# Two-layer gated cross-attention with experts: causal maxima in shared banks, one-hots by wide comparisons, two casts on ScalarE

## The reference

```python
x = x + tanh(g_xattn[0]) * L0_xattn(layernorm(x), ctx, ctx, mask, ...)  # 16 heads of 16, causal
x = x + tanh(g_ffn[0])   * L0_ffn(layernorm(x), ...)    # 32 experts, top 8, capacity 256
x = x + tanh(g_xattn[1]) * L1_xattn(layernorm(x), ctx, ctx, mask1, ...) # 16 heads, not causal
x = x + tanh(g_ffn[1])   * L1_ffn(layernorm(x), ...)    # 8 experts, top 2, capacity 1024

def L0_xattn(q, k, v, ...):
    scores = einsum('bhqd,bhkd->bhqk', q @ Wq + bq, k @ Wk + bk) / 4
    scores = where(tril(ones(S, S)), scores, finfo.min) + attention_mask
    return einsum('bhqk,bhkd->bhqd', softmax(scores), v @ Wv + bv) @ Wp + bp
```

## Time and profile before

| | |
|---|---|
| median of three runs | 2179.87 us (2171.82 to 2183.06) |
| the profiled execution's own time | 2182.45 us |
| its span in the profile | 2180.7 us |
| mean granted clock of TensorE | 0.923 of full speed |
| layer 0's attention, first to last maximum (L823) | 79.6 to 597.1 us |
| layer 1's attention, first score for maxima to last (L658) | 1021 to 1559 us |
| DVE sat idle for PE before L823 | 113.0 us |
| PE sat idle for DVE's L823 | 35.9 us |

### The profile page before, as it was taken

One profiled execution on the slowest core, in us unless ns is written; L12 is line 12 of the kernel. 1 busy time (PEld: TensorE's weight loads), 2 busy tenths in 40 slices (PEclk: granted clock), 3 DMA queues, 4 the chain that ended last, 5 costly groups with the idle time before them and its releaser, 6 DMA issues. The chain is left out here.

```text
span 2180.7 us, 30480 instructions
## 1 busy us (share of the span) xinstructions
PE 1843.1 (85%) x9979; PEld 1024.6 (47%) x9979; DVE 1138.2 (52%) x3758; ACT 862.8 (40%) x1780; POOL 598.0 (27%) x577
## 2 busy tenths in 40 slices
PE   2689899888872999916899999998971999999995
PEld 1345455444442777613334444443331566666664
DVE  3477778877855344433877877777521111112211
ACT  1356555555450322203376766665650111111110
POOL 1312111210001577723211331231112233333322
PEclk9799999998985999958899999999985999999998
DMA  3445454335221678733333324332013233333314
GB/s 93 151 123 160 130 168 130 112 98 160 72 72 46 158 169 170 141 66 113 120 98 113 116 83 120 114 106 67 32 49 84 83 76 76 74 77 78 70 27 97
DMA packets 204252, 222.88 MB, mean 102 GB/s; under 512 B 33438, under 2 KB 195231, under 8 KB 203431
## 3 DMA queue, kind: packets, MB, share of 16 engines
q1 hardware_dynamic: 176458, 177.48, 26.5%
q0 software_dynamic: 27648, 43.60, 10.7%
HBM read 155.06 MB, written 86.93 MB: 111 GB/s over the span
## 5 line engine op out<-in xcount | busy, mean ns | idle before, releaser
L710 ACT ACTIVATE pt<-stb 128x512 f32<-128x512 f32 (+3 forms) x1024 | 498.6, 520 | 345.8 <-PE stb L671 190.8
L658 PE MATMUL mxb<-kst,qst 96*128 96x512 bf16 (+4 forms) x1024 | 358.7, 356 | 65.3 <-DVE nmx L823 35.9
L827 DVE TENSOR_REDUCE nmx<-mxb 128x1 f32<-128x512 f32 x512 | 341.2, 685 | 123.6 <-PE mxb L658 113.8
L668 PE MATMUL stb<-qst,kst 99*128 99x512 bf16 (+4 forms) x1024 | 351.8, 351 | 11.9 <-ACT pt L710 8.7
L823 DVE CUSTOM_DVE_ANT_0 masked<-mxb,hide 128x128 bf16<-128x128 f32 (+3 forms) x512 | 242.1, 487 | 116.2 <-PE mxb L658 113.0
L682 PE MATMUL ob<-pt,va 128*32 128x512 f32 (+3 forms) x2048 | 240.4, 542 | 1.4 <-ACT pt L710 1.1
L1387 PE MATMUL e_h_bank<-e_xT,e_w 128*128 128x512 f32 x512 | 224.7, 597 | 6.1 <-ACT e_xT L1427 5.4
L1401 PE MATMUL e_y_bank<-e_w,e_h 128*128 128x256 f32 x1024 | 226.9, 379 | 0.0
L668 PEld LDWEIGHTS stb<-qst,kst 102*128 102x128 bf16 (+1 forms) x1024 | 101.4, 100 | 234.4 <-ACT pt L710 148.2
L1401 PEld LDWEIGHTS e_y_bank<-e_w,e_h 128*128 128x128 f32 x1024 | 192.9, 190 | 31.8 <-issue 7.2
L1084 POOL TENSOR_TENSOR qk<-qk,parts 128x512 f32<-128x512 f32 x64 | 72.9, 1161 | 449.9 <-ACT qk L743 229.1
(11 more groups left out here) (224 smaller groups left out, 2494.8 us busy)
## 6 DMA issues: line engine op xcount, KB each, us to landing
qk_parts<-parts SPq DMA_DIRECT2D x16, 1536.0 KB, 5.9
qst<-qk_parts SPq DMA_DIRECT2D x384, 64.0 KB, 2.3
kst<-qk_parts SPq DMA_DIRECT2D x384, 64.0 KB, 2.2
e_w<-in_L_ffn_w SPq DMA_DIRECT2D x16, 1024.0 KB
rows<-rows SPq DMA_DIRECT2D x15, 1060.0 KB, 8.5
crow<-in_ctx SPq DMA_DIRECT2D x16, 512.0 KB
x_after_l<-xres SPq DMA_DIRECT2D x16, 512.0 KB, 3.3
e_gu_nat<-in_L_ffn_gate_up_proj SPq DMA_DIRECT2D x64, 128.0 KB
```

The source lines that it names most:

```text
L658: pe.matmul(out[:, 0:nk], qst[par][0:rows_used, h, qt * P:(qt + 1) * P], kst[par][0:rows_used, h, 0:nk], start=True, stop=True).then_inc(s ...
L668: last = pe.matmul(out[:, q0:S], kst[par][0:ROWS, h, kt * P:(kt + 1) * P], qst[par][0:ROWS, h, q0:S], start=True, stop=not causal)
L710: act.activation(pt[:, u % 8, q_from(kt):S], stb[(STEPS * b + u) % N_ST][:, q_from(kt):S], ACT.Exp, scale=SCALE).then_inc(s["st_free"], 1)
L827: dve.tensor_reduce(nmx[:, qt, h:h + 1], got, AX.X, ALU.max, negate=True).then_inc(s["max_free"], 1)
```

## The change

1. **Shared banks.** In layer 0 the score tiles for the maxima of two heads lie in 5 full banks of 512 columns instead of 8 partly filled ones: query tiles 0 and 2 of a head together (128 + 384), tile 3 alone (512), and tile 1 of both heads together (256 + 256). That is 40 banks an item. PE fills a bank in the steps 0, 2, 3, 5 and 7 of each 8. DVE reduces with plain TENSOR_REDUCE: one for a tile, or one for both halves of 256.
2. **Masks as matmuls.** Behind each of the 64 score matmuls of an item, PE adds the causal mask to the last 128 columns with a matmul of the identity and `hide_max` (128 x 128), as L671 does for the transposed scores. `hide` (128 x 512) and the four `masked` tiles are gone.
3. **One-hots.** `one_hot` has four pieces: two TENSOR_TENSOR comparisons of 512 columns (4 x 128) for `lo1`, one of 512 columns (8 x 64) for `hv`, and one TENSOR_SCALAR of 512 columns that multiplies by the token's number, behind a new semaphore `hchain`. The 16 pieces of an item stand in 16 different steps.
4. **Two casts on ScalarE.** `middle` (two activations of 512 columns for each side) and `shift_out` move from DVE to ACT, in both layers, in the same steps; ACT's `norm2_apply` moves two steps later.
5. **Table.** `list` trips go from 18, 20, 22, 24 to 18, 20, 25, 28 and `enlist` from 25 to 29; `x` from 27, 28 to 24, 31; the first `o` from 26 to 27 and into the other bank, `normalise` with it from 26 to 28, `norm2_mean` from 28 to 29. The table holds for both layers.

```diff
-    c.hide = sb(c, ctx, "hide", [P, S], BF16)
+    c.hide_max = sb(c, ctx, "hide_max", [P, P], BF16)
...
-    18: ("list", -2, 0, 0, 0), 20: ("list", -2, 0, 1, 0), 22: ("list", -2, 0, 2, 0), 24: ("list", -2, 0, 3, 0), 3: ("k", 2, 0, 0, 0), 4: ("k", 2, 0, 1, 0), 5: ("shift", 0, 1, 0, 1),
+    3: ("k", 2, 0, 0, 0), 4: ("k", 2, 0, 1, 0), 5: ("shift", 0, 1, 0, 1),
+    18: ("list", -2, 0, 0, 0), 20: ("list", -2, 0, 1, 0), 25: ("list", -2, 0, 2, 0), 28: ("list", -2, 0, 3, 0),
...
-    26: ("o", 0, 0, 0, 0), 27: ("x", 3, 0, 0, 1), 28: ("x", 3, 1, 0, 0), 32: ("v", 2, 0, 0, 1), 35: ("v", 2, 0, 1, 1),
+    24: ("x", 3, 0, 0, 1), 27: ("o", 0, 0, 0, 1), 31: ("x", 3, 1, 0, 0), 32: ("v", 2, 0, 0, 1), 35: ("v", 2, 0, 1, 1),
...
+ONE_HOT_AT = (1, 4, 6, 7, 9, 10, 12, 14, 19, 20, 21, 22, 23, 24, 25, 26)
+
+
+def whole_banks():
+    return {u: ((u // NT, u % NT, 0),) for u in range(STEPS)}
+
+
+def shared_banks():
+    banks = {}
+    for h in range(0, HEADS, 2):
+        u = NT * h
+        banks[u] = ((h, 0, 0), (h, 2, P))
+        banks[u + 2] = ((h, 3, 0),)
+        banks[u + 3] = ((h, 1, 0), (h + 1, 1, 2 * P))
+        banks[u + 5] = ((h + 1, 0, 0), (h + 1, 2, P))
+        banks[u + 7] = ((h + 1, 3, 0),)
+    return banks
...
             def maxima(n, u):
-                wait(pe, s["max_free"], STEPS * n + u - N_MX + 1)
-                nk = k_to(qt)
-                out = mxb[(STEPS * n + u) % N_MX]
-                pe.matmul(out[:, 0:nk], qst[par][0:rows_used, h, qt * P:(qt + 1) * P],
-                          kst[par][0:rows_used, h, 0:nk], start=True, stop=True).then_inc(s["max_full"], 1)
+                if u not in MAX_BANKS:
+                    return
+                no = N_MAX * n + MAX_NO[u]
+                wait(pe, s["max_free"], no - N_MX + 1)
+                for h, qt, at in MAX_BANKS[u]:
+                    out, nk = mxb[no % N_MX][:, at:at + k_to(qt)], k_to(qt)
+                    last = pe.matmul(out, qst[par][0:rows_used, h, qt * P:(qt + 1) * P], kst[par][0:rows_used, h, 0:nk],
+                                     start=True, stop=not causal)
+                    if causal:
+                        last = pe.matmul(out[:, nk - P:nk], c.identb[:, :], c.hide_max[:, :], start=False, stop=True)
+                last.then_inc(s["max_full"], 1)
...
+            def middle(n, side):
+                act.wait_ge(s[("rest_q", "rest_k")[side]], n + 1)
+                wait(act, s["parts_out"], 16 * n)
+                for cc in range(NC):
+                    last = act.activation(parts[:, side, 1, cc, :], qk[:, side, cc, :], ACT.Copy)
+                last.then_inc(s[("mid_q", "mid_k")[side]], 1)
+
+            def shift_out(n, hf):
+                act.wait_ge(full["shift"], 2 * n + hf + 1)
+                wait(act, s[f"shift_in{hf}"], 48 * n)
+                act.activation(m3T[hf][:, :], bank_of("shift", hf)[0:3 * HALF, :], ACT.Copy).then_inc(evac["shift"], 1)
...
             def maxima(n, u):
-                if causal:
-                    wait(dve, s["max_free"], STEPS * n + u - 3)
-                    dve.tensor_tensor_reduce(out=masked[u % 4][:, 0:k_to(qt)], in0=got, in1=c.hide[:, S - k_to(qt):S], scale=-1.0,
-                                             scalar=LARGEST, op0=ALU.add, op1=ALU.min,
-                                             accum_out=nmx[:, qt, h:h + 1]).then_inc(s["max_free"], 1)
+                if others and others[0][1] == qt:
+                    last = dve.tensor_reduce(nmx[:, qt, h:h + 2], got[:, 0:2 * k_to(qt)].rearrange("p (h k) -> p h k", h=2),
+                                             AX.X, ALU.max, negate=True)
                 else:
-                    dve.tensor_reduce(nmx[:, qt, h:h + 1], got, AX.X, ALU.max, negate=True).then_inc(s["max_free"], 1)
+                    for h, qt, at in MAX_BANKS[u]:
+                        last = dve.tensor_reduce(nmx[:, qt, h:h + 1], got[:, at:at + k_to(qt)], AX.X, ALU.max, negate=True)
+                last.then_inc(s["max_free"], 1)
...
-            def one_hot(b, t):
-                for k in range(8):
-                    dve.tensor_scalar(lo1[t % 2][:, k, :], c.lanes[:, :], lo_f[:, t, k:k + 1], None, ALU.is_equal)
-                for k in range(8):
-                    last = dve.tensor_scalar(hv[t % 2][:, k, :], c.lanes[:, 0:N_HI], hi_f[:, t, k:k + 1], c.tok1[:, 0:1],
-                                             ALU.is_equal, ALU.mult)
+            def one_hot(b, t, piece):
+                if piece < 2:
+                    ks = slice(4 * piece, 4 * piece + 4)
+                    dve.tensor_tensor(lo1[t % 2][:, ks, :], c.lanes[:, :].unsqueeze(1).to_broadcast([P, 4, P]),
+                                      lo_f[:, t, ks].unsqueeze(2).to_broadcast([P, 4, P]), ALU.is_equal)
+                elif piece == 2:
+                    dve.tensor_tensor(hv[t % 2][:, :, :], c.lanes[:, 0:N_HI].unsqueeze(1).to_broadcast([P, 8, N_HI]),
+                                      hi_f[:, t, :].unsqueeze(2).to_broadcast([P, 8, N_HI]), ALU.is_equal).then_inc(s["hchain"], 1)
+                else:
+                    dve.wait_ge(s["hchain"], 4 * b + t + 1)
+                    dve.tensor_scalar(hv[t % 2][:, :, :], hv[t % 2][:, :, :], c.tok1[:, 0:1], None, ALU.mult).then_inc(s["lo_rdy"], 1)
```

More of the change, by code:

```diff
@@ L246, in attention @@
     HALF = HEADS // 2
+    MAX_BANKS = shared_banks() if causal else whole_banks()
+    N_MAX = len(MAX_BANKS)
+    MAX_NO = {u: i for i, u in enumerate(sorted(MAX_BANKS))}
     with ExitStack() as ctx:
@@ L650, in maxima @@
             def maxima(n, u):
[L651 removed]
+                par = n % 2
                 rows_used = STACK + 3 if causal else STACK
@@ L776, in _ @@
             for it in ITERATIONS:
-                prev, cur, n3 = item(it, -1), item(it, 0), item(it, 3)
+                prev, cur, nxt, nn, n3 = (item(it, k) for k in range(-1, 4))
                 for u in range(STEPS):
@@ L780, in _ @@
                         exps(cur, u)
+                    if u == 3 and nn is not None:
+                        middle(nn, 0)
+                    if u == 21 and nn is not None:
+                        middle(nn, 1)
+                    if u == 6 and cur is not None:
+                        shift_out(cur, 1)
+                    if u == 37 and nxt is not None:
+                        shift_out(nxt, 0)
                     if u in (16, 17, 18, 20) and n3 is not None:
                         norm1_apply(n3, (16, 17, 18, 20).index(u))
-                    if u in (31, 32, 33, 34) and prev is not None:
-                        norm2_apply(prev, u - 31)
+                    if u in (33, 34, 35, 36) and prev is not None:
+                        norm2_apply(prev, u - 33)
                     if u == 3 and prev is not None:
@@ L843, in shift_part @@
                     dve.tensor_tensor(nmx[:, :, heads], nmx[:, :, heads], m3[hf][:, :, r, :], ALU.subtract).then_inc(link, 1)
-            def shift_out(n, hf):
-                dve.wait_ge(full["shift"], 2 * n + hf + 1)
-                wait(dve, s[f"shift_in{hf}"], 48 * n)
-                dve.tensor_copy(m3T[hf][:, :], bank_of("shift", hf)[0:3 * HALF, :]).then_inc(evac["shift"], 1)
             def normalise(b, g):
@@ L1007, in _ @@
                         shift_part(cur, 1, u)
-                    if u == 3 and nn is not None:
-                        middle(nn, 0)
-                    if u == 6 and cur is not None:
-                        shift_out(cur, 1)
                     if u == 8 and prev is not None:
@@ L1029, in _ @@
                         shift_part(nxt, 0, u - 32)
-                    if u == 37 and nxt is not None:
-                        shift_out(nxt, 0)
                     if u == 39 and cur is not None:
```

44 lines of the change are left out of this document (18 added, 26 removed).

## The result

The changed kernel takes **2144.77 us** (median of 4 runs, 2143.32 to 2148.58), the kernel before 2180.21 us beside it: ratio 0.9846, 95% interval 0.9817 to 0.9876, 35 us less. The forecast was 2147. The profiled execution has a span of 2142.8 us, 37.9 less than before.

A forecast was written before the change was run, and what follows sets the result against it. PE was taken as the bound, except in steps 8 to 31 of layer 0, where DVE ends the waits. Terms summing to -32.9 us took the profiled 2182.45 to 2149.5, and 2.6 less for the median gave 2147; range 2120 to 2172.

The forecast's parts named there:

- The bound: Attention phases: DVE ends PE's waits in steps 8 to 31 of layer 0 (34.8 us in iteration 3); PE bounds elsewhere.
- The sum: Whole kernel: changes forecast by iteration, layer 0's tail and layer 1 add up to -32.9 us.
- The tail: End of layer 0, 645.7 to 702.0: only DVE's chain with 8 one-hot tiles, forecast -4.5 us.
- The relief of DVE: Layer 0: one-hots 3.0, `shift_out` 1.2, `middle` 1.4, maxima 0.6; DVE spared 6.2 us an iteration.
- lag 3 steps instead of 2: Layer 0's maxima: a shared bank holds 1.6 steps, so two banks let DVE fall 3 steps behind; no separate size.
- the table: Moved trips: no work added, and `x` at 31 waits for `enlist` at 29; put at nothing.
- The masks: Layer 0 on PE's path: 64 mask matmuls an item at 0.06 us, 3.8 us an iteration, 8 items.
- The waits: Layer 0, iterations 2 to 6: PE still waits 2.6 us an iteration, twice iteration 1's 1.3.
- Rival B: DVE stays the bound in layer 0's steps 8 to 31, or wide one-hots win nothing; -14, 2166 us; chance 0.18.
- Rival C: ScalarE becomes the bound in steps 3 to 8, both layers: 3.6 us an iteration, 2194 us; chance 0.12 with Rival D.
- Rival D: Layer 0's mask matmuls cost their full length, 0.22 us each: +82 us; next to no chance, counted with Rival C.
- Rival A: More is won: DVE never holds PE up, layer 1 loses nothing, tail gains 3 more; -53.4, 2126 us; chance 0.12.

The follow-up runs named there:

- narrow_block: The changed kernel with one-hots as before: 16 narrow comparisons a tile, all in one step, new table kept; 2173.10 us, ratio 0.9970.
- four_buffers: The changed kernel with four one-hot buffers instead of two and pieces in earlier steps; 2127.16 us beside 2166.13 for the kernel before, ratio 0.9816.
- old_maxima: The changed kernel with layer 0's maxima as before: 64 banks, masks in DVE's reduction; 2119.80 us beside 2166.13 for the kernel before, ratio 0.9778.

## Why the prediction was right, and where its reasons were not

**The bound** held: steps 8 to 31 of layer 0 are where the time was. They take 27.4 us (28 to 31 forecast) at a clock of 1.00, and are no longer one stretch: PE sets steps 16 to 23, DVE steps 24 to 31.

**The sum** met its parts: iterations 2 to 4 at 201.1 (200.7 forecast), iteration 5 at 63.9 (62.5), iteration 6 at 58.3 (56.9), iteration 1 +2.7 (+3.8), iterations -1 and 0 together +1.5 (+4), iteration 7 -3.0 (-2). The tail, up to the writing of `token`, fell by 4.6 us (-4.5). A one-hot tile takes 2.20 us. Layer 1, from its first score for maxima to its last exponential, was put at +3 and is 4.4 us shorter: the casts cost it nothing, and its last iteration won 3.4. Against that, 5.4 us of layer 0's gain were lost again in the experts behind it (first gather to layer 1's first score: 323.2 us, 317.8 before), which the prediction did not look at. From the first gather to layer 1's first exponential, the traces of the fourteen kernels have from 368 to 382 us, so this is the experts' own scatter as far as is known. That these two misses nearly cancel is luck, and part of why the total came within 3 us.

**The relief of DVE** is the step whose reasoning failed, although its total did not. It added up 6.2 us over all steps and all four parts, as if a microsecond were worth the same anywhere. Taken back one by one from the changed kernel, the casts (2.6 us) and the shared banks (0.6 us and "lag 3 steps instead of 2") cost nothing that can be told; the one-hots, sized at 3.0 of 6.2, cost 27 us, because two of their four tiles run into the steps in which DVE also has `add_residual`, `norm2_stats` and `enlist`. These prices don't add up to shares of the gain. The masks alone lose 13 to 15.5 us, and with them narrow_block is still 6.5 us faster than the kernel before; so by this sum casts, banks and table give some 20 us with the old comparisons in place, in steps 8 to 23 above all. The prediction put the table at nothing, and no run tests that. The right question was when DVE is late, not how long it is busy: after the change it is late in steps 24 to 31, and by 0.7 us at `rank`, and it was four_buffers, which moved work out of steps 24 to 31, that shortened them without a loss elsewhere.

**The masks** were priced well, 3.8 us an iteration against 2.7 to 3.3, and the relief that they buy too (none but the 0.6). Side by side in the working the two terms said that this part loses, and the prediction did not draw that conclusion: about 15 us were being given away.

**The waits**, 2.6 us an iteration, came out at (201.1 - 191.5) / 3 = 3.2, as waits at the three trips named above, not as slips at the maxima banks.

**Rival B** fell in both its forms: the wide comparison costs 0.68 us where it meets nothing, as the earlier trace rows had it, and going back to narrow ones costs more than any other part. The estimate by the rates of the Trainium skill's page *VectorE: DVE Perf Modes* (*The perf-mode tier table*), 0.4 us a tile narrow and 1.7 wide, has the order wrong for these sizes; the tile takes 2.95 and 2.20. **Rival C** fell: ACT is now busy for 8.0 of 8.2 us in steps 0 to 7 of layer 0, yet in iterations 2 to 4 PE waited 0.5 us in all for its copies, and layer 1 did not get slower. Its price had a slip: 50 less 2.6 and 3 is 45, so 2192 and not 2194. **Rival D** fell at 0.04 to 0.05 us a mask. **Rival A** (2126) was not reached. old_maxima comes to 2132, by a way that the rival didn't name: the masks stay on DVE.

## What to carry to other kernels

Before an engine is relieved, find the steps in which it is late: 2 us an iteration taken off in steps with slack moved nothing, 1.7 us moved out of the late steps gave 1.8. When a change consists of several parts, price each on both sides by itself, since a good total can hide a part that loses 15 us. A wait that goes away when a trip is moved is only gone if the steps behind it have not grown, and the other layer that uses the same table has not either.
